# Fewer operand rows for the maximum, ones rows by transfer, and five emptying transfers moved into the projection

## The reference, cut to what matters

```python
q, k, v = proj(Wq, bq, norm(x)), proj(Wk, bk, ctx), proj(Wv, bv, ctx)   # 16 heads of 8 features
q, k = rotary(q), rotary(k)                  # all three seen as (8, 16, 256): feature, head, position
prob = softmax(einsum('bdhn,bdhm->bhnm', q, k) / sqrt(8))               # 256 x 256 per head and block
x = x + Wm @ einsum('bhnm,bdhm->bdhn', prob, v) + bm
x = x + experts0(norm(x))                    # 64 experts, 8 for each token, rows gathered by expert
...
```

## Time and profile before

| what | value |
|---|---|
| time of the kernel before, median of 3 runs | 696.23 us (695.4 to 699.45) |
| span of the profiled execution | 736.3 us |
| projection, from the start to PE's first matmul of the attention | 65.0 us |
| attention, to PE's last matmul before the experts | 65.0 to 277.8 us |
| mean granted PE clock over the span | 0.820 |

### The profile page before, as it was taken

One profiled execution on the slowest core, in us unless ns is written; L12 is line 12 of the kernel. 1 busy time (PEld: TensorE's weight loads), 2 busy tenths in 40 slices (PEclk: granted clock), 3 DMA queues, 4 the chain that ended last, 5 costly groups with the idle time before them and its releaser, 6 DMA issues.

```text
span 736.3 us, 12068 instructions
## 1 busy us (share of the span) xinstructions
PE 506.3 (69%) x3519; PEld 380.2 (52%) x3519; DVE 381.7 (52%) x1235; ACT 221.4 (30%) x578; POOL 350.0 (48%) x476
## 2 busy tenths in 40 slices
PE   1723886977787530699899891467743988988870
PEld 1621442443343220688787780346632977878760
DVE  8964564786776351244444442898750333333336
ACT  0450263554456410333332320244421211112110
POOL 9493110254645453265555543034447656665540
PEclk9975597798889655799999995597775999999995
DMA  5189896766467497789999524921126988888937
GB/s 172 32 190 293 290 283 230 188 162 159 141 207 239 153 351 285 225 257 340 330 312 305 188 73 149 410 93 59 61 73 205 343 272 297 262 279 275 311 130 278
DMA packets 82915, 163.95 MB, mean 223 GB/s; under 512 B 13070, under 2 KB 58142, under 8 KB 81072
## 3 DMA queue, kind: packets, MB, share of 16 engines
q1 hardware_dynamic: 56832, 106.20, 44.8%
q0 software_dynamic: 13968, 32.29, 11.9%
q10 hardware_dynamic: 12064, 24.84, 11.5%
HBM read 104.94 MB, written 66.78 MB: 233 GB/s over the span
## 4 chain that ended last, share of the span: by engine, by line
PE 28%; DMA 10%; issue 8%; DVE 6%; another core or an unknown queue 3%; POOL 2%; ACT 1%; SPq 1%; POOLq 0%; DVEq 0%; ACTq 0%
PE sc_ps L1756 10%; PE hd_ps_up L1212 5%; DMA hd_side<-held 4%; PE sc_ps L1738 4%; DMA sc_rows<-rows 2%; POOL rows L1359 2%; DMA rows<-hd_side_out,hd_side_target 2%; PE hd_ps_out L1218 2%; PE hd_ps_x L1190 1%; PE sc_ps L1694 1%; PE sc_ps L1706 1%; PE sc_ps L1746 1%; DVE sc_rows L1845 1%; DMA sc_tile_rows<-listed 1%
## 5 line engine op out<-in xcount | busy, mean ns | idle before, releaser
L987 DVE TENSOR_REDUCE at_top<-at_ps_top 128x2 f32<-128x512 f32 x128 | 83.4, 683 | 62.3 <-PE at_ps_top L898 54.8
L1359 POOL DMA_INDIRECT rows<-hd_out,hd_rows x64 | 62.2, 972 | 63.6 <-DVE hd_out L1310 37.6
L1756 PE MATMUL sc_ps<-sc_t_turned,e_w 128*112 128x128 f32 x672 | 87.7, 285 | 2.5 <-issue 2.3
L1059 ACT ACTIVATE at_prob<-at_ps_score 128x512 f32<-128x512 f32 x128 | 72.4, 593 | 54.9 <-PE at_ps_score L916 43.2
L1756 PEld LDWEIGHTS sc_ps<-sc_t_turned,e_w 128*112 128x112 f32 x672 | 85.0, 188 | 5.9 <-issue 2.8
L1212 PE MATMUL hd_ps_up<-hd_x_turned,e_arena 128*128 128x160 f32 x512 | 83.0, 306 | 0.2 <-ACT hd_x_turned L1272 0.2
L1212 PEld LDWEIGHTS hd_ps_up<-hd_x_turned,e_arena 128*128 128x128 f32 x512 | 76.5, 193 | 9.3 <-issue 6.2
L682 POOL DMA_INDIRECT held<-e_extended,e_address x64 | 63.0, 984 | 32.7 <-issue 18.9
L898 PE MATMUL at_ps_top<-e_arena 96*128 96x256 bf16 x256 | 59.9, 325 | 25.5 <-PEq L107 22.0
L682 POOL DMA_INDIRECT listed<-e_extended,e_address x32 | 33.6, 1049 | 68.1 <-DVE e_address L674 60.6
L916 PE MATMUL at_ps_score<-e_arena 99*128 99x256 bf16 x256 | 56.0, 311 | 12.1 <-DMA e_arena<-at_top_rows 8.0
(11 more groups left out here) (266 smaller groups left out, 933.3 us busy)
## 6 DMA issues: line engine op xcount, KB each, us to landing
e_w<-in_weights SPq DMA_DIRECT2D x42, 704.0 KB
e_arena<-in_weights SPq DMA_DIRECT2D x52, 384.0 KB
held<-e_empty ACTq DMA_DIRECT2D x16, 960.0 KB, 6.9
hd_rows<-held SPq DMA_DIRECT2D x15, 768.0 KB
sc_rows<-rows SPq DMA_DIRECT2D x8, 1024.0 KB, 13.7
sc_tile_rows<-listed SPq DMA_DIRECT2D x42, 144.0 KB
parts<-op_parts SPq DMA_DIRECT2D x8, 576.0 KB
e_arena<-in_weights ACTq DMA_DIRECT2D x12, 384.0 KB
```

What stands on the lines that cost most here:

```text
L987: nc.vector.reduce_max(top[:, 2 * h:2 * h + 2], ps_top[at % TOPS][:], AX_X).then_inc(top_found, 1)
L1059: nc.scalar.activation(prob[at % RING][:], ps_score[at % SCORES][:], ACT.Exp, scale=scale).then_inc(prob_ready, 1)
L1359: nc.gpsimd.indirect_dma_start(rows_out, to, out_ap, None, bounds_check=TOKENS * LAYER0.chosen - 1, oob_is_err=False).then_inc(semaphore, 16)
L1756: op = nc.tensor.matmul(ps_up[u % 2][:, part, c * P:(c + 1) * P], up_w[u][:, k, at:at + W], t_turned[u % 2][:, k, :], start=k == 0, stop=k ...
```

## The change

`TOP` becomes 48, so the operand matrices have 51 rows in place of 99, and nothing has to be cleared. k's three ones rows are no longer filled by POOL: POOL writes a 3 x 128 tile of ones, and SP copies it into all four buffers by four transfers behind the input loads (`place_ones`); PE waits for them before the first `score`. POOL's eight memsets of v stay, but the last four wait until DVE has turned the weights. ACT issues the dummy and the first five emptying transfers at the start of the projection, as soon as x and ctx have landed; the other eleven go out in the attention, from step -20 to step 20.

```diff
-TOP = 96
+TOP = STACK
...
-    def set_rows(self, nc, pool, n):
-
-        nc.gpsimd.memset(self.k[n][0:TOP].bitcast(F32), 0.0)
-        nc.gpsimd.memset(self.q[n][0:TOP].bitcast(F32), 0.0).then_inc(self.rows_set, 1)
-        pool.wait_ge(self.rows_set, 2 * n + 1)
-        nc.gpsimd.memset(self.k[n][TOP:ROWS].bitcast(F32), ONES_PAIR).then_inc(self.rows_set, 1)
-        pool.wait_ge(self.rows_set, 2 * n + 2)
+    def place_ones(self, engine):
+
+        engine.wait_ge(self.ones_known, 1)
+        for n in range(DEEP):
+            to = self.k[n][TOP:ROWS, :].bitcast(F32).rearrange("a (r n) -> a r n", n=P)
+            engine.dma_start(to, self.ones[:].unsqueeze(1).broadcast_to([PARTS, H * D // 2 // P, P])).then_inc(self.ones_placed, 16)
...
-        if b < DEEP:
-            engine.wait_ge(self.rows_set, 2 * (b + 1))
...
             setup.sp_load(sp)
+            operands.place_ones(sp)
...
             nc.gpsimd.memset(held.empty[:], SKIP_FLOAT).then_inc(held.empty_set, 1)
+            nc.gpsimd.memset(operands.ones[:], ONES_PAIR).then_inc(operands.ones_known, 1)
             for b in range(B):
+                if b == B // 2:
+                    pool.wait_ge(w_ready, 1)
                 nc.gpsimd.memset(operands.v[:, b], 1.0).then_inc(ones_set, 1)
-            for n in range(2):
-                operands.set_rows(nc, pool, n)
...
-                if b == 3:
-                    operands.set_rows(nc, pool, 2)
...
+            act.wait_ge(x_loaded, 16)
+            act.wait_ge(c_loaded, 16)
+            for g in range(Held.AHEAD):
+                held.act_empty(act, g)
...
+    AHEAD = 5
...
-            operands.set_rows(nc, pool, DEEP - 1)
...
+                if at == 0:
+                    pe.wait_ge(operands.ones_placed, 16 * DEEP)
...
-                if at % 4 == 0 and 0 <= (at + LEAD) // 4 < GROUPS:
-                    held.act_empty(act, (at + LEAD) // 4)
+                g, late = divmod(at + LEAD, 4)
+                if late == 0 and Held.AHEAD + g < GROUPS:
+                    held.act_empty(act, Held.AHEAD + g)
```

More of the change, by code:

```diff
@@ L185, in __init__ @@
         self.loaded = [s.sem(f"loaded{n}") for n in range(DEEP)]
-        self.rows_set = s.sem("rows_set")
-    def set_rows(self, nc, pool, n):
-        nc.gpsimd.memset(self.k[n][0:TOP].bitcast(F32), 0.0)
-        nc.gpsimd.memset(self.q[n][0:TOP].bitcast(F32), 0.0).then_inc(self.rows_set, 1)
-        pool.wait_ge(self.rows_set, 2 * n + 1)
-        nc.gpsimd.memset(self.k[n][TOP:ROWS].bitcast(F32), ONES_PAIR).then_inc(self.rows_set, 1)
-        pool.wait_ge(self.rows_set, 2 * n + 2)
+        self.ones = s.sbuf("ones", [PARTS, P], F32)
+        self.ones_known, self.ones_placed = s.sem("ones_known"), s.sem("ones_placed")
+    def place_ones(self, engine):
[3 more added lines that the diff above has]
+            engine.dma_start(to, self.ones[:].unsqueeze(1).broadcast_to([PARTS, H * D // 2 // P, P])).then_inc(self.ones_placed, 16)
     def load(self, engine, b):
         n = b % DEEP
-        if b < DEEP:
-            engine.wait_ge(self.rows_set, 2 * (b + 1))
         engine.wait_ge(self.stored[b % self.OUT], 16 * (b // self.OUT + 1))
```

## The result

The changed kernel takes 738.64 us (738.34 to 739.26), the kernel before 695.82 in the same comparison: ratio 1.059, 95% interval 1.0545 to 1.0635, slower. The forecast was 683.6.

What follows compares the result with a forecast made beforehand. Bound by when each stage of the first 140 us ends: opening, DMA-held end of projection, PE's waits for placed rows. -6.8 - 1.1 - 5.5 = -13.4 on 736.3 gives 722.9, times 0.9456 is 683.6 us; range 674 to 693.

Steps and rivals of the forecast that it cites:

- 48 rows: PE's attention matmuls: 96 rows take what 99 take, so cutting to 48 and 51 was costed at nothing.
- slower: the clock with half the rows: Rival: PE's attention never granted 2.4 GHz with 48 and 51 rows; 50 us lost, 731 us; chance 0.07.
- gains of 13.4: Sum of the gains at the opening, block 3's load and step 24: -6.8 - 1.1 - 5.5 us.
- three signs of being wrong: ACT still issuing when the first cut is due; barrier above 62; granted clock 0.50 in stretches without waits.
- The opening, -6.8 us: Start of the projection: with memsets off DVE's way the rotary loop starts at 17.1, moving the barrier by -6.8 us.
- This cover: Projection: ACT's emptying issues, 5 to 7 us, end before its first cut at about 19.5; 0 to 3.3 us lost.
- only where POOL pauses for a semaphore: Opening: DVE gets through POOL's memsets only at such pauses, its scaling of block 0 taking 6.06 us.
- Step 24, -5.5: Attention: without three emptying transfers ahead, the placed rows land at 117.2 in place of 122.7, shortening PE's wait.
- Block 3's load, -1.1: Attention's start: SP goes on 5.4 us earlier, so PE's first wait for placed rows, 1.12 us, goes.
- The sum without the rows: Whole kernel: the forecast gain of -13.4 us on the traced span, with the row cut itself costed at nothing.

Runs made afterwards that it cites:

- rows96: The changed kernel with 96 rows for the maximum and 99 for the score again, rows cleared by POOL memsets: 688.75 us, ratio 0.986.
- rows48_alone: The kernel before with only the cut to 48 and 51 rows and ones placed by transfer, as many memsets, no emptying moved: 745.95 us, ratio 1.067.
- warm128x4: The changed kernel with PE's warm-up made of 96 matmuls of 128 rows in place of 24 of 48 rows: 738.54 us.
- best5: The changed kernel with 96 and 99 rows, buffers 0 to 2 filled by ACT before its emptying issues, buffer 3 by POOL: 681.85 us, ratio 0.980.
- rows96_ahead0: rows96 with no emptying transfer in the projection, all issued in the attention as before the change: 694.12 us, ratio 0.996.
- rows64: rows96 with 64 rows for the maximum and 67 for the score: 753.98 us, ratio 1.080.
- top48_score99: rows96 with only the matmuls for the maximum at 48 rows, the score left at 99: 736.02 us, ratio 1.055.

## Why the prediction was wrong, point by point

- *"48 rows. No instruction fewer on PE, and the same columns ... so I cost this at nothing."* This step failed. The durations of 96 and 99 rows that it leaned on were rows of one clock, and the row count acts on the clock: 0.50 for 0.87. `rows96` and `rows48_alone` show it from both sides; at the same level the matmuls take the same time with half the rows (0.43 us above).
- *The rival "slower: the clock with half the rows"* named mechanism, place and sign; 731 was forecast and 738.6 measured. Its price of 50, taken between 35 and 70, is 47 after the prediction's scaling, and 49.4 was measured. It was added to gains of 13.4 (12.7 scaled) of which only 5.6 to 7.3 showed (`rows48_alone`), since a PE at the lower clock no longer waits in step 24. A chance of 0.07 was too small for a term with no row on either side. Of the three signs of being wrong 0.50 in stretches without waits came. ACT's issues ended 0.2 us before the first cut was due, and the barrier opened below 62.
- *The opening, -6.8 us*: right in DVE (17.02). The barrier gained 5.2. The other 1.6 fit the 1.5 us by which ACT's first cut is late. Its issues held it 7.4 us (5 to 7 forecast; five took 6.95 where four took 4.01 in the earlier trace rows), until 19.21; the cut was due at 19.40, when DVE's first sum was ready. This cover was called thin, but the prediction left out the table load and v's first copy, which stood between them. In `warm128x4`, whose projection is the same, five took 5.62, the first cut was not late, and the attention began at 58.58. `best5`, with the load ahead, has it begin at 57.28. As this start scatters by 1.2 us, the loss is not shown to be ACT's alone.
- *DVE gets through "only where POOL pauses for a semaphore"*: not so throughout. In before DVE's turned bias ends at 15.71 (13.92 + 1.79), between POOL's memsets of lines 190 (to 15.66) and 191 (from 15.60), which no semaphore parts. What sets the length of these waits stays open.
- *Step 24, -5.5*: right in its cause (`rows96_ahead0`), somewhat larger in size where the clock is up (6.94 to 0.35), and worth nothing at 0.50: there `rows48_alone`, which moves no emptying, does not wait for the placed rows either. The share of 0.84 from 116 to 123, for which the prediction names, is in the trace of before but not in these rows.
- *Block 3's load, -1.1*: not to be read at 0.50. In `best5`, where buffer 3 is filled ahead of the barrier, the wait at step 0 is gone, but one of 1.33 us comes at 91.93.
- *The sum without the rows*: with 96 rows the same edits give -10.8 us (688.75 against 699.51), and -14.2 where the fill is out of the way (681.85 against 696.01); -12.6 was forecast.

The Trainium skill (TensorE: Matmul & The Clock Gate, Part 1: The HAM clock gate) ties the clock to how busy PE has been. PE's busy time in the profile would by itself have it the other way here: 156.77 us of 164 at 0.50, 129.15 at 0.87.

The runs don't settle why fewer rows lose the level; that zero rows are enough to hold it shows only that the added rows need no content.

## What to carry to other kernels

Zero rows of a contraction are not waste until the granted clock has been looked at: before an operand is cut down, ask whether any row shows PE at the upper level with so few rows; if none does, the price is the difference between the whole stage at one level and at the other (here 49.4 us, a third of the stage), and its chance should not be set small. When PE's busy share rises and its waits vanish while fewer matmuls are done in a stretch, read the clock column first. Put fills on an idle engine beside which the critical one is seen to run at full speed: here ACT (DVE's operation took 0.17 us) instead of POOL (5.45).

## What I had not expected of the hardware

- The clock is lost by row counts while PE hardly stops. From 86 to 250 us it is 0.50 with 48 or 64 rows, 0.56 with 80, 0.85 with 96, and 0.87 with 96 and 128 in the score.
- At one clock, steps differ with the pairing of rows. `rows64` (64 and 67 rows) is 15 us slower than after at the same 0.50, and 12.3 of these lie between the first and the last exponential (212.2 us for 199.9). From one pair of matmuls to the next it takes 0.54 us, where after takes 0.43:

```profile
150.19 0.61 PE L933 MATMUL at_ps_score<-e_arena 67*128 67x256 bf16 x2
150.73 0.61 PE L913 MATMUL at_ps_top<-e_arena 64*128 64x256 bf16 x2
```

From 86 to 250 us its weight loads for the maximum take 107 ns, and PEld idles:

```profile
L913 PEld LDWEIGHTS at_ps_top<-e_arena 64*128 64x128 bf16 x186 | 11.9, 107 | 38.0 <-issue 36.4 <-DVE at_top L1004 1.6
```

In after the same group, with 48 and 51 rows in turn, reads:

```profile
L900 PEld LDWEIGHTS at_ps_top<-e_arena 48*128 48x128 bf16 x196 | 29.0, 148 | 12.8
```

The traced execution of `top48_score99` looks like `rows64` (PEld 43.86 us busy of 164; 69.13 in after). In both, one matmul of a step has at most 64 rows and the other more; whether that is the cause was not tried.
